# Eight PSUM banks shared out anew: three for attention scores, two for transposed samples and probabilities

## The reference

```python
x = x + deformable_conv(groupnorm(x), offset_w, offset_b, conv_w)   # 3x3, nine taps, bilinear samples
t = to_tokens(x)                                                     # (8, 3136, 128)
q, k, v = ln(t) @ Wq.T, ln(t) @ Wk.T, ln(t) @ Wv.T
t = t + softmax(where(causal, q @ k.T * 128**-0.5, -inf)) @ v        # one head, causal
t = t + expert_choice_ffn(ln(t), gate_w, gate_b, weight1, weight2)   # 64 experts, top 8 tokens each
x = from_tokens(t)
```

## Time and profile before

| | us |
|---|---|
| median of 3 runs | 3207.58 |
| lowest, highest | 3206.52, 3216.11 |
| the profiled execution, its own time | 3214.02 |
| its span, first to last instruction | 3212.2 |
| TensorE busy | 2880.1 (90%) |
| VectorE, ScalarE, GpSimd busy | 1898.5, 1828.8, 1764.4 |
| TensorE clock granted, mean | 0.957 |

### The profile page before, as it was taken

The page is one execution under the profiler, slowest core; times in us unless marked ns, Lnnn a source line. Parts: engine busy times, 40 slices in busy tenths (PEclk is TensorE's granted clock), DMA queues, the critical chain, the costliest instruction groups (busy, mean ns, idle before and its releaser), DMA issues. The chain is left out here.

```text
span 3212.2 us, 53916 instructions
## 1 busy us (share of the span) xinstructions
PE 2880.1 (90%) x19490; PEld 2195.3 (68%) x19490; DVE 1898.5 (59%) x7142; ACT 1828.8 (57%) x4004; POOL 1764.4 (55%) x1815
## 2 busy tenths in 40 slices
PE   4588999999999999999999999999999998999555
PEld 2466776777777777677777776777767776777432
DVE  1456664766576664766477664766486657564324
ACT  1355665666566665666566665666566666664220
POOL 1777764775467654775467644765477556710000
PEclk9699999999999999999999999999999999999787
DMA  5634333552255333643255333633255324411397
GB/s 148 200 112 129 116 112 108 144 139 86 87 153 154 94 96 105 159 119 104 88 136 154 94 90 110 170 110 102 84 148 158 89 81 110 117 66 43 118 341 282
DMA packets 265861, 405.97 MB, mean 126 GB/s; under 512 B 44681, under 2 KB 175977, under 8 KB 265083
## 3 DMA queue, kind: packets, MB, share of 16 engines
q0 software_dynamic: 86400, 236.04, 26.4%
q1 hardware_dynamic: 175323, 153.11, 15.7%
q10 hardware_dynamic: 3872, 13.37, 1.0%
HBM read 368.42 MB, written 85.35 MB: 141 GB/s over the span
## 5 line engine op out<-in xcount | busy, mean ns | idle before, releaser
L495 POOL DMA_INDIRECT shared<-pair_table,idx x1800 | 1752.2, 973 | 1061.5 <-issue 524.6
L1041 PE MATMUL bank_o<-vals,prob_t 128*128 128x128 f32 x5200 | 701.0, 280 | 50.5 <-ACT prob_t L531 49.0
L531 ACT ACTIVATE prob_t<-bank_r 128x512 f32<-128x512 f32 (+3 forms) x728 | 394.9, 547 | 609.6 <-PE bank_r L1028 607.4
L751 DVE CUSTOM_DVE_ANT_0 prob<-bank_s,mask 128x512 f32<-128x512 f32 (+3 forms) x728 | 453.8, 631 | 456.9 <-PE bank_s L1019 453.5
L1041 PEld LDWEIGHTS bank_o<-vals,prob_t 128*128 128x128 f32 x5200 | 637.4, 193 | 84.1 <-ACT prob_t L531 73.7
L1019 PE MATMUL bank_s<-keys,qt 128*128 128x512 f32 (+3 forms) x1456 | 661.4, 560 | 17.4 <-DVE cmax L751 17.4
L518 ACT ACTIVATE shared<-shared,wa 128x128 f32<-128x128 f32 x1800 | 564.2, 390 | 75.9 <-DMA shared<-pair_table,idx 75.9
L741 DVE SCALAR_TENSOR_TENSOR shared<-shared,wb 128x128 f32<-128x128 f32 x1800 | 502.3, 346 | 118.1 <-ACT shared L518 117.4
L1005 PEld LDWEIGHTS bank_conv<-convw_t,smp_t 128*128 128x128 f32 x3600 | 460.1, 200 | 97.8 <-ACT smp_t L524 56.7
L1005 PE MATMUL bank_conv<-convw_t,smp_t 128*128 128x128 f32 x3600 | 497.2, 286 | 32.3 <-ACT smp_t L524 32.2
L1028 PE MATMUL bank_r<-ident,prob 128*128 128x128 f32 x2600 | 417.3, 279 | 1.8 <-ACT prob L598 1.8
(11 more groups left out here) (155 smaller groups left out, 2315.2 us busy)
## 6 DMA issues: line engine op xcount, KB each, us to landing
pair_table<-in_dram SPq DMA_DIRECT2D x224, 224.0 KB
shared<-in_dram SPq DMA_DIRECT2D x32, 1024.0 KB, 9.2
shared<-pair_table,idx POOLq DMA_INDIRECT x1800
shared<-in_dram SPq DMA_DIRECT2D x8, 1568.0 KB
t<-in_dram SPq DMA_DIRECT2D x48, 256.0 KB
t_dram<-t SPq DMA_DIRECT2D x48, 256.0 KB
stage<-t_dram SPq DMA_DIRECT2D x8, 832.0 KB, 6.8
pm_dram<-logit SPq DMA_DIRECT2D x8, 800.0 KB, 6.6
```

Of the source, the lines that this page charges most:

```text
L495: pool.indirect_dma_start(g[t % RING][:, n, :], None, pair_table[b % 2], bass.IndirectOffsetOnAxis(ap=idx[:, b % 2, i * TAPS + n:i * TAPS ...
L531: act.activation(prob_t[q % 2][:, 0:w], ring_bank(("prob", t, c))[:, 0:w], ACT.Copy)\
L751: dve.tensor_tensor_reduce(prob_at(t, k0, w), bank_s[q % 2][:, 0:w], m, 1.0, NEG, ALU.add, ALU.max, cmax[t % 2][:, c:c + 1]).then_inc(scor ...
L1041: last = pe.matmul(attn_ps, prob_t[q % 2][:, n * P:(n + 1) * P], vals[:, slot(tb, at), :], start=(at == 0), stop=(at == ti))
```

## The change

`bank_s` gets three banks and `bank_r` two. Everything else follows from this: a scores matmul waits for the chunk three before it and not two; a transpose group waits for the group two before it in the ring and not three. No instruction is added or removed but for waits, and no order is changed. The setup at the start, which transposes the convolution weights through `bank_r`, also goes round two banks.

```diff
-        bank_s = [psum(f"bank_s{r}") for r in range(2)]
-        bank_r = [psum(f"bank_r{r}") for r in range(3)]
+        bank_s = [psum(f"bank_s{r}") for r in range(3)]
+        bank_r = [psum(f"bank_r{r}") for r in range(2)]
@@ def ring_bank(use):
-            return bank_r[RING_AT[use] % 3]
+            return bank_r[RING_AT[use] % 2]
@@ setup on ScalarE
-                act.activation(convw_t[:, n, :], bank_r[n % 3][:, 0:P], ACT.Copy).then_inc(setup_ev, 1)
+                act.activation(convw_t[:, n, :], bank_r[n % 2][:, 0:P], ACT.Copy).then_inc(setup_ev, 1)
@@ def keep_scores(t, c):
-                dve.tensor_tensor_reduce(prob_at(t, k0, w), bank_s[q % 2][:, 0:w], m, 1.0, NEG, ALU.add, ALU.max,
+                dve.tensor_tensor_reduce(prob_at(t, k0, w), bank_s[q % 3][:, 0:w], m, 1.0, NEG, ALU.add, ALU.max,
@@ def free_ring(use):
-                if k >= 3:
-                    what, t, n = RING_ORDER[k - 3]
+                if k >= 2:
+                    what, t, n = RING_ORDER[k - 2]
@@ setup on TensorE
-                after(setup_ev, 1 + n - 2 if n >= 3 else 0)
-                pe.transpose(bank_r[n % 3][:, 0:P], raw_conv.rearrange("o (c t) -> o c t", t=TAPS)[:, :, n], ident[:])\
+                after(setup_ev, 1 + n - 1 if n >= 2 else 0)
+                pe.transpose(bank_r[n % 2][:, 0:P], raw_conv.rearrange("o (c t) -> o c t", t=TAPS)[:, :, n], ident[:])\
@@ def scores(c):
-                    after(score_ev, q - 1)
+                    after(score_ev, q - 2)
-                    pe.matmul(bank_s[q % 2][:, 0:w], qt[k % 2][:, at:at + P], key_chunk(tb, k0, w),
+                    pe.matmul(bank_s[q % 3][:, 0:w], qt[k % 2][:, at:at + P], key_chunk(tb, k0, w),
```

## The result

| | before | changed |
|---|---|---|
| median, us | 3207.05 | 3580.46 (3575.72 to 3581.46, 4 runs) |
| ratio | | 1.1155, 95% interval 1.1132 to 1.1177 |
| span of the profiled execution | 3212.2 | 3579.6 |
| mean granted TensorE clock | 0.957 | 0.942 |

What follows compares the result with a forecast made beforehand. TensorE was taken to set the pace from the second image to the last. Waits less the scores' gain, 315 us, plus 90 for the clock made 405; 3207.6 + 405 = 3613, rounded 3610, range 3500 to 3690.

Steps and rivals of the forecast that it cites:

- The bound and the rigid shift: TensorE sets the pace from second image to last; the rest of each step moves along, so nothing is given back.
- half is won back: Rival: half the loss is regained later in the step through probability evictions and row maximum; 3400 us, chance 0.08.
- The end is unchanged: Sign of a right forecast: the last 245 us of the kernel stay as they were.
- The ring: With two transpose banks, the third group waits for the first sample eviction behind ACT's exponential; 51.3 us read per image.
- some 190 waits of 330 to 400 us: Sign of a right forecast: a new TensorE wait at the transposes for ACT's eviction, with this count and total.
- 0.1 us for each restart: Added for about 170 restarts of an emptied TensorE queue, as a matmul starts 0.11 us after its weight load: 17 us.
- The scores: With three banks the third score chunk no longer waits for DVE: a gain of 4.5 us per image, about 33.
- The clock: TensorE's clock falls to the 1.2 GHz level after long waits: 64 falls at 1.4 us, 90 us, bounds 0 and 150.
- The 75 waits: Waits at ten positions in seven images and five in the eighth; three in four, 56, taken to bring a clock fall.
- The sum: Ring waits less the scores' gain over eight images, corrected at first and last image, plus restarts: 315 us.
- The rival without a falling clock: Rival: the ring's waits come but the clock holds; 3523 us, chance 0.22.
- The other side: Rival: DVE ends the row maximum earlier, the exponential precedes its step, only the scores' 33 us gain remains; 3175, chance 0.04.

Runs made afterwards that it cites:

- run 1: Changed kernel with scores back to two banks, ring of two kept, one bank unused: 3584.11 us, ratio 1.1182.
- run 2: Changed kernel with the third transpose group issued later on TensorE, after the first score chunks and misc E, just ahead of `products(0)`: 3171.00 us, ratio 0.9885.
- run 3: Changed kernel with the first sample eviction put ahead of the exponential in ACT's order: 3261.05 us, ratio 1.0156.
- run 5: Two runs: run 4 with two scores banks, 3502.48 us; the kernel before with the late third group of run 2, 3217.98 us.
- run 4: Changed kernel with matmuls of constants ahead of the third transpose group, filling TensorE's wait for the eviction: 3479.76 us, ratio 1.0852.
- run 6: Run 2 with two evictions ahead of the exponential, 3139.63 us; run 2 with constant matmuls at tiles 23 and 24, 3151.66; kernel before, three evictions ahead, 3199.82.

## Why the prediction was right

- **The bound and the rigid shift.** TensorE set the pace, and a microsecond in which it stood still was lost. ACT's chain kept its distance from the step to 0.01 us (tile 18, 3.00 and 3.00, and so in all 25 tiles of a middle image), so next to nothing was given back later: the wait of TensorE for the probability evictions went from 49.0 to 44.3 us, and its wait for the gate's logits (L959) from 24.0 to 17.4. The rival "half is won back" fell by this. The end is unchanged, as forecast: from the start of the last step with samples on, the kernel takes 340.0 us before and 338.5 after.
- **The ring.** Forecast were some 190 waits of 330 to 400 us; there are 193 with 377. An image in the middle has 50.5 us of them, where 51.3 were read. The estimate of 0.1 us for each restart was near: group 2 starts 0.14 us after the eviction's end where 0.05 was read before. At tile 18 that end is 1654.57 + 0.57. Runs 1, 2 and 3 show this wait as the cause, and the exponential as its length.
- **The scores.** Forecast 33, measured 23 with the clock level (run 5), 4 in the change itself. The prediction read the gain in a kernel in which DVE comes late; behind the ring's wait it does not, and 0.20 us in each longer step is left.
- **The clock.** This is the term that was mis-sized: 90 forecast, some 63 by run 4's mean price (139 us at 0.45), 70 at the 0.50 of single steps. The new falls as such were sized about right, partly by luck. The 75 waits that the prediction counts are those of tiles 9, 10, 13, 14 and 17 to 22, as far as its list tells (it names waits of 2.1 us or more, and of these the list has eleven positions, not ten); 52 of them brought a low stretch, where 56 were taken, and the shorter waits brought none, where 8 were taken. At 1.7 us each, not 1.4, the 52 cost 88. What the forecast left out are falls that the kernel before has and the change has not: the low level went from 61 to 48 us at tiles 23 and 24, from 68 to 55 elsewhere in the steps, and from 147 to 134 outside them, 39 us or, by the mean price, some 18 of time; 88 less 18 is 70. So the steps have 23 low stretches before and 70 after, 47 more and not 64, and the mean clock is 0.942 and not 0.90 to 0.93.
- **Where the clock falls.** The prediction took three waits in four at each position, and the trace has all or none: in the second to the sixth image they come at tiles 13, 14, 18, 19, 20, 21 and 23 each time, once more at 9 or 10, and never at 17, 22 and 24, whose waits are as long (2.8, 2.2 and 3.5 us). The section of the Trainium skill quoted in the prediction (TensorE: Matmul & The Clock Gate) tells of a clock that swings when TensorE idles often and briefly; it does not say that each wait brings a fall, and the prediction read it so. The trace agrees with the swinging, and has a fall behind 60 of the 193 waits.
- **The sum.** 373 less 63 is 310 for the waits less the scores, beside 315. The rival without a falling clock (3523) is out, since the clock did fall. Run 4 bears its size out: with the wait filled the kernel takes 3480, and with the kernel before's low level, 81 us more at 0.45, it would take some 3516.
- **The other side.** The exponential did not move further ahead of its step (at tiles 11 and 12 of a middle image 0.97 and 1.56 us ahead, before and after), so the case of a faster kernel had no place to begin. What makes the third bank pay is cover for the ring (run 2) and an earlier eviction (run 6), 3171 and 3140 us.

## What to carry to other kernels

Before a ring is shortened, find for each user the eviction that it will wait for, and what stands ahead of that eviction in its engine's queue: here one exponential of 0.4 to 3 us. Then count the work that lies between the new wait and the point where the result was wanted before; that is the cover that is lost, and moving the waiting group behind it gives it back. A bank's worth can be read only with such waits out of the way: a third scores bank gave 4 us beside the wait, and 47 without it even though the ring gave up a bank for it there.

## What the runs showed of the hardware

- An idle TensorE can cost twice: once for the wait, and again when the clock falls to the 1.2 GHz level behind it. Work of no use in the wait gained 100 of 3580 us (run 4). A low stretch of 3.4 us cost 1.7 us in the steps of the middle images, dearer than the 1.4 that I had read.
- Whether a wait of such a length brings the fall depends on where it lies, not on its length alone: 2.8 us at tile 17 never did so in the middle images, 2.9 at tile 18 always. The waits of tiles 9 and 10 are 1.9 and 2.0 us in every full image but the first; in the second image the fall comes at tile 9, in the fourth at tile 10 (steps of tiles 9 and 10, first in the one and then in the other; the clock is the third number from the end):

```profile
699.24:715.27 16.03, 13.09 (x74) 8.96 (x73) 9.80 (x41) 8.22 (x19) 9.38 (x10) 0.89 0.77 193
715.27:729.46 14.19, 12.11 (x82) 9.46 (x80) 7.17 (x26) 9.69 (x21) 8.29 (x8) 1.00 0.22 66
1511.51:1525.90 14.39, 11.45 (x75) 8.45 (x74) 9.68 (x41) 8.22 (x19) 9.01 (x10) 1.00 0.84 214
1525.90:1541.78 15.88, 13.80 (x81) 10.04 (x80) 7.16 (x26) 9.69 (x21) 8.86 (x10) 0.89 0.29 85
```

- A small edit moves the falls as well as their number: filled waits at tiles 23 and 24 took ten low stretches away there and three came at tile 5 (run 6). How the place decides was not tested.
